# Two matrix products of a graph kernel put into one region, with a shared ring of parts and another order of the second product's tiles

## The chip, the cores and the metric

The kernel runs on one core of one Trainium2 chip. The metric is the device time of one execution in microseconds (us). Three runs of the kernel before gave 911.8, 912.16 and 915.66 us, median 912.16 us.

## What is computed

`x` is 2048 x 512, `adj` is 2048 x 2048, all in fp32. The part of the reference that matters here:

```
def _L0_gnn_ref(x, Coefficient2, A):        # called as _L0_gnn_ref(h, adj, adj)
    def adjacent_mat(adj):
        adj = adj + jnp.eye(adj.shape[0])
        deg = jnp.sum(adj, axis=1)
        dinv = jnp.where(deg > 0, deg ** (-0.5), 0.0)
        return dinv[:, None] * adj * dinv[None, :]
    adj = adjacent_mat((A + A.T) * 0.5)
    y = Coefficient2 @ adj
    y = y @ x
    return y

h = jnp.maximum(_layernorm(x, axis=-1), 0.0)
x = x + _L0_gnn_ref(h, adj, adj)
h = jnp.maximum(_layernorm(x, axis=-1), 0.0)
x = x + _L1_gnn_ref(h, adj, L1_gnn_W, ...)   # 8 heads of masked attention, then four dense layers
return x
```

The kernel takes `Coefficient2 @ (A_norm @ h)` from the right: the **first product** is G = A_norm h (2048 x 512), with A_norm = dinv (A + A.T + 2I)/2 dinv, and the **second product** is adj @ G. Adding `x` to it gives `x1`, which the projection to the heads and the attention use.

## The kernel before, in words

**Tiles.** All 2048-row arrays are 16 tiles of 128 rows (T = 16). Both products sum over 16 tiles, and each is made in two halves of eight output tiles, because eight PSUM banks of 128 x 512 hold eight output tiles (`bank[0..7]`, G8 = 8). A **step** is one tile of the sum times the eight output tiles of a half. To hold fp32 accuracy each factor is split in a high and a low part of type fp32r, and a step is 8 banks x 3 matmuls (lines 73, 74 and 75: high by high, high by low, low by high), 24 matmuls of 128 x 512. Each product has 32 steps.

**Ring of parts.** A step needs four tiles: the high and the low part of the 128 x 1024 rows (`s_hi`, `s_lo` in the first product, `a_hi`, `a_lo` in the second) and of the 128 x 512 tile on the other side (`x_hi`, `x_lo`; `g_hi`, `g_lo`). Each has two buffers, so that the parts of step s+1 are cut while PE works on step s. ACT cuts `s_hi` and `x_hi` (lines 516 and 522) and `a_hi` (748); DVE cuts `s_lo` and `x_lo` (289, 295), `g_hi`, `g_lo` and `a_lo` (816, 818, 821) and writes the 0/1 mask of the rows (823). A step's parts may be cut once the step two before it is done (`slot_free`).

**First product** (`smooth_features`). 20 steps are run while `adj` and its transpose come in. Steps 20 to 31 (`FIRST_LATE` to `STEPS - 1`) need only what lies in SBUF: the tiles `kept` (12 tiles) and `kept_end` (4). The banks of the tiles 8 to 15 of G are taken out at step 20 (line 474), those of the tiles 0 to 7 at the end (line 494). Each is one DVE instruction for one bank, and the one for bank k may run when PE has finished the last step's three matmuls into bank k.

**Border.** Each product is a region of its own (`nc.Block()`): all engines meet at its end, and the second one's code begins after that. The second region's SBUF tiles lie where the first one's were.

**Second product** (`spread_and_project`). The row tiles of the transpose come through `rows`, which has four places (SLOTS = 4). The first four tiles are loaded by the end of the first product's queue. SP (the engine that issues the loads here) first issues x's second load (4 MB, line 717), the weights (719) and two vectors (723), and then, for each further row tile, waits until its place is free (line 729: the mask of the tile four before is done) and loads it (line 87). The tiles are taken in the order 0, 1, ..., 15 in both halves, so step 0 needs tile 0 of G. After the last step of each half DVE adds x to the banks (line 830).

After that come the second layer norm, the projection, and attention with the dense layers, none of which the diff touches.

Of the kernel before, what the change touches and what calls it, by code (L numbers as in the profile page):

```python
# [37 lines left out]
P = 128  # L38
# [63 lines left out]
def smooth_features(nc, bank, ident, G, rows, rows_loaded, x, adj, adj_t):  # L102
# [5 lines left out]
    with ExitStack() as ctx:  # L108
        def sb(name, shape, dt=F32):
            return ctx.enter_context(nc.sbuf_tensor(name, shape, dt))  # L110

        def sem(name):
            return ctx.enter_context(nc.semaphore(name))

        EARLY = SLOTS
        FIRST_NOW = 2 * EARLY
        FIRST_LATE = T + EARLY
        STEPS = 2 * T
        CHUNKS = ((0, 4), (4, 8), (8, 12), (12, 16))
        h = sb("l0_h", [P, T, F])  # L120
        now = sb("l0_now", [P, SLOTS, GW])
        with nc.sbuf_tensor("l0_early_hi", [P, EARLY, F], F32R) as early_hi, \
                nc.sbuf_tensor("l0_early_lo", [P, EARLY, F], F32R) as early_lo:
            pass
        kept_end = sb("l0_kept_end", [P, SLOTS, GW])
        kept = sb("l0_kept", [P, T - SLOTS, GW])
        rows_k = sb("l0_rows_k", [P, SLOTS, GW])
        s_hi = sb("l0_s_hi", [P, 2, GW], F32R)
        s_lo = sb("l0_s_lo", [P, 2, GW], F32R)
        x_hi = sb("l0_x_hi", [P, 2, F], F32R)  # L130
        x_lo = sb("l0_x_lo", [P, 2, F], F32R)
        base = now[:, 0:2, 0:F]
        stats = sb("l0_stats", [P, 4, 6])
        mv = sb("l0_mv", [P, T, 2])
        var = sb("l0_var", [P, T])
        root = sb("l0_root", [P, T])
        rstd = sb("l0_rstd", [P, T])
        nmr = sb("l0_nmr", [P, T])
        tmp = sb("l0_tmp", [P, T])
        part = sb("l0_part", [P, T, 2])  # L140
        deg = sb("l0_deg", [P, T, 1])
        pos = sb("l0_pos", [P, T, 1])
        degc = sb("l0_degc", [P, T, 1])
        droot = sb("l0_droot", [P, T, 1])
        y = sb("l0_y", [P, T, 1])
        ytmp = sb("l0_ytmp", [P, T, 1])
        dinv = sb("l0_dinv", [P, T, 1])
        hdinv = sb("l0_hdinv", [P, T, 1])

        def kept_half(i):  # L150
            return kept[:, i, :] if i < T - SLOTS else kept_end[:, i - T + SLOTS, :]

        ident_zeroed = sem("ident_zeroed")
        x_loaded = [sem(f"l0_x_loaded{c}") for c in range(len(CHUNKS))]
        sums_loaded = [sem(f"l0_sums_loaded{b}") for b in range(SLOTS)]
        first_loaded = sem("l0_first_loaded")
        ln_chain = sem("l0_ln_chain")
        var_ready = sem("l0_var_ready")
        ln_root = sem("l0_ln_root")
        norm_ready = sem("l0_norm_ready")  # L160
        h_ready = sem("l0_h_ready")
        summed = sem("l0_summed")
        inv_chain = sem("l0_inv_chain")
        deg_ready = sem("l0_deg_ready")
        root_ready = sem("l0_root_ready")
        hi_ready = sem("l0_hi_ready")
        lo_ready = sem("l0_lo_ready")
        x_hi_ready = sem("l0_x_hi_ready")
        x_ready = sem("l0_x_ready")
        slot_free = sem("l0_slot_free")  # L170
        acc_done = sem("l0_acc_done")
        part_kept = sem("l0_part_kept")
        base_ready = sem("l0_base_ready")
        g_done = sem("l0_g_done")
        INV = 4
        DEG = 3

        def half_of(i, at_once):
            left = (i < EARLY) == at_once
            return slice(0, GW) if left else slice(GW, N)  # L180

        def step_source(s):
            if s < EARLY:
                return now[:, s, :]
            if s < FIRST_NOW:
                return kept_half(s - EARLY)
            if s < FIRST_LATE:
                return now[:, (s - EARLY) % SLOTS, :]
            return kept_half(s - T)

        def x_of(s):

            if s < EARLY:
                return s, s, early_hi[:, s, :], early_lo[:, s, :]
            return (s - EARLY if s < FIRST_LATE else s - T), s - EARLY, x_hi[:, s % 2, :], x_lo[:, s % 2, :]

        def wait_for_sum(eng, s, k):

            group = (EARLY - 1, FIRST_LATE - 1, STEPS - 1).index(s)
            if k < G8 - 1:  # L200
                eng.wait_ge(acc_done, (G8 - 1) * group + k + 1)
            else:
                eng.wait_ge(slot_free, s + 3)

        with nc.Block() as block:
            @block.sync
            def _(sp):
                def load_x(c):
                    lo, hi = CHUNKS[c]
                    sp.dma_start(h[:, lo:hi, :], x[lo * P:hi * P, :].rearrange("(t p) f -> p t f", p=P)  # L210
                                 ).then_inc(x_loaded[c], 16)

                def load(i):
                    b, tile = i % SLOTS, slice(i * P, (i + 1) * P)
                    first, second = half_of(i, True), half_of(i, False)
                    if i >= SLOTS:
                        before = i - SLOTS
                        sp.wait_ge(deg_ready, DEG * before + 1)
                        sp.wait_ge(lo_ready, (before if before < EARLY else before + EARLY) + 1)
                    sp.dma_start(rows[:, b, :], adj_t[tile, first]).then_inc(rows_loaded[b], 16)  # L220
                    sp.dma_start(now[:, b, :], adj[tile, first]).then_inc(sums_loaded[b] if i else first_loaded, 16)
                    sp.dma_start(rows_k[:, b, :], adj_t[tile, second]).then_inc(sums_loaded[b], 16)
                    sp.dma_start(kept_half(i), adj[tile, second]).then_inc(sums_loaded[b], 16)

                load_x(0)
                for i in range(EARLY + 2):
                    load(i)
# [12 lines left out]
            def _(v):  # L240
                links = {}

                def link(*name):

                    links[name] = len(links) + 1

                def statistics(c):
                    lo, hi = CHUNKS[c]
                    v.wait_ge(x_loaded[c], 16)
                    for t in range(lo, hi):  # L250
                        v.bn_stats(stats[:, t - lo, :], h[:, t, :]).then_inc(ln_chain, 1)
                        link("stats", t)

                def variances(c):
                    lo, hi = CHUNKS[c]
                    for k in range(hi - lo):
                        v.wait_ge(ln_chain, links["stats", lo + k])
                        v.bn_aggr(mv[:, lo + k, :], stats[:, k, :]).then_inc(ln_chain, 1)
                        link("mv", lo + k)
                    v.wait_ge(ln_chain, links["mv", hi - 1])  # L260
                    v.tensor_scalar(var[:, lo:hi], mv[:, lo:hi, 1], EPS, None, ALU.add).then_inc(var_ready, 1)

                def refine(c, n):

                    part_of = slice(*CHUNKS[c])
                    d, at, yy, to = var[:, part_of], root[:, part_of], rstd[:, part_of], tmp[:, part_of]
                    if n == 0:
                        v.wait_ge(ln_root, c + 1)
                        v.reciprocal(yy, at).then_inc(ln_chain, 1)
                        link("refined", c, 0)  # L270
                        return
                    v.wait_ge(ln_chain, links["refined", c, n - 1])
                    if n == 1:
                        v.tensor_tensor(to, yy, yy, ALU.mult).then_inc(ln_chain, 1)
                    elif n == 2:
                        v.tensor_tensor(to, to, d, ALU.mult).then_inc(ln_chain, 1)
# [72 lines left out]
                for n in range(6):  # L349
                    refine(0, n)  # L350
# [1714 lines left out]
```

## Time and profile before

| | |
|---|---|
| profiled execution | 911.92 us |
| its span in the profile | 910.0 us |
| median of three runs | 912.16 us |
| PE busy | 860.6 us (95% of the span) |
| DVE busy | 691.3 us (76%) |
| ACT busy | 411.6 us (45%) |
| POOL busy | 274.9 us (30%) |
| mean granted TensorE clock | 0.983 |

PE is TensorE's matmuls, PEld its weight loads, DVE VectorE, ACT ScalarE, POOL GpSimd and SP SyncE. Times in a row are us from the start of the span. A clock of 1.00 is 2.4 GHz, the upper of two levels; the lower is 1.2 GHz. A PE row's start is measured and its end is modelled, so the pace of matmuls is read from the starts. Tile names stand without their numbers (`l_a_hi` is `l1_a_hi`), and `x` can be the tile `x1`.

### The profile page before, as it was taken

To read this page: it belongs to the slowest core of one execution; us is meant where nothing else is said; L and a number is where in the kernel's file an instruction comes from. 1 tells how busy PE (TensorE), PEld (TensorE's weight loads), DVE (VectorE), ACT (ScalarE), POOL (GpSimd) and SP (SyncE) were. 2 spreads that over 40 slices of the span, in tenths; PEclk is the share of its full clock that TensorE was granted. 3 is DMA by queue.
4 is the path that set the end of the run, shared out by engine and by line. 5 is a ranking of instruction groups with operands and counts; after the bars stand their busy time and mean duration, and the time that the engine had idled before them with its cause. 6 is when DMAs were issued, how large, how long until landed. Compare 5 with 4: busy or idle time off the path is not lost.

```text
span 910.0 us, 15449 instructions
## 1 busy us (share of the span) xinstructions
PE 860.6 (95%) x5144; PEld 754.7 (83%) x5144; DVE 691.3 (76%) x1192; ACT 411.6 (45%) x742; POOL 274.9 (30%) x287
## 2 busy tenths in 40 slices
PE   2999999989999999999599999999999999998997
PEld 1787888868888888778399999999999999997553
DVE  6788985564557775677899999999999999996622
ACT  3535423311111221245286666666666656773331
POOL 0000000000000000066646555555555544573111
PEclk9999999999999999999699999999999999999999
DMA  9969820029232321310050000010010032001142
GB/s 353 406 212 340 351 93 1 0 82 279 100 95 90 113 95 46 126 61 4 26 200 25 23 23 26 25 23 23 24 25 23 23 93 71 13 2 47 46 138 96
DMA packets 36115, 87.36 MB, mean 96 GB/s; under 512 B 7072, under 2 KB 7968, under 8 KB 36064
## 3 DMA queue, kind: packets, MB, share of 16 engines
q1 hardware_dynamic: 35024, 82.46, 26.5%
q0 software_dynamic: 1040, 4.26, 1.2%
q8 instruction: 27, 0.44, 0.2%
q14 instruction: 24, 0.20, 0.1%
HBM read 73.93 MB, written 12.78 MB: 95 GB/s over the span
## 4 chain that ended last, share of the span: by engine, by line
PE 46%; DVE 2%; POOL 1%; ACT 1%; issue 1%; ACTq 0%; POOLq 0%; DVEq 0%
PE bank L1558 25%; PE bank L1582 13%; PE bank L2011 3%; DVE l_q L1243 2%; PE bank L73 1%; PE bank L75 1%; PE bank L74 1%; PE bank L1994 1%; PE bank L2003 1%; PE bank L1973 1%; DVE wh L1924 0%; POOL l_parts L1477 0%; POOL l_o_q L1470 0%; ACT l_mask L1356 0%; POOL l_o_m L1489 0%
## 5 line engine op out<-in xcount | busy, mean ns | idle before, releaser
L1243 DVE SCALAR_TENSOR_TENSOR l_q<-bank,neg_d,mask 128x512 fp32r<-128x512 f32 x512 | 338.7, 742 | 28.2 <-PE bank L1558 27.4
L1558 PE MATMUL bank<-l_parts,l_q 128*128 128x260 f32 x2048 | 253.3, 285 | 8.4 <-DVE l_q L1243 8.4
L1558 PEld LDWEIGHTS bank<-l_parts,l_q 128*128 128x128 f32 x2048 | 250.9, 191 | 8.5 <-issue 8.5
L803 POOL TENSOR_TENSOR l_prod<-wh,l_a 128x512 f32<-128x512 f32 x30 | 36.6, 1240 | 401.2 <-ACT wh L773 401.2
L1356 ACT ACTIVATE l_mask<-mask 128x512 fp32r (+1 forms) x256 | 136.4, 619 | 0.2
L1582 PE MATMUL bank<-l_parts,l_mask 128*128 128x260 f32 x1024 | 129.0, 286 | 0.8 <-ACT l_o_q L1362 0.8
L1582 PEld LDWEIGHTS bank<-l_parts,l_mask 128*128 128x128 f32 x1024 | 127.1, 189 | 1.1 <-ACT l_o_q L1362 1.0
L73 PE MATMUL bank<-l_g_hi,l_a_hi 128*128 128x512 f32 x256 | 100.6, 393 | 4.4 <-DVE l_a_lo L821 4.1
L74 PE MATMUL bank<-l_g_lo,l_a_hi 128*128 128x512 f32 x256 | 100.3, 392 | 0.0
L748 ACT ACTIVATE l_a_hi<-rows 128x1024 fp32r<-128x1024 f32 x32 | 33.9, 1062 | 146.4 <-PE bank L75 123.9
L75 PE MATMUL bank<-l_g_hi,l_a_lo 128*128 128x512 f32 x256 | 100.1, 391 | 0.0
L1362 ACT ACTIVATE l_o_q<-bank 128x260 f32<-128x260 f32 x128 | 49.4, 388 | 105.9 <-PE bank L1558 97.8
L73 PE MATMUL bank<-l_x_hi,l_s_hi 128*128 128x512 f32 x192 | 74.9, 390 | 0.4 <-DVE l_x_lo L295 0.4
L74 PE MATMUL bank<-l_x_lo,l_s_hi 128*128 128x512 f32 x192 | 74.7, 389 | 0.0
L75 PE MATMUL bank<-l_x_hi,l_s_lo 128*128 128x512 f32 x192 | 74.7, 389 | 0.0
L73 PEld LDWEIGHTS bank<-l_g_hi,l_a_hi 128*128 128x128 f32 x256 | 48.4, 189 | 15.7 <-issue 5.6
L816 DVE CAST l_g_hi<-G 128x512 fp32r (+1 forms) x32 | 13.7, 427 | 60.8 <-PE bank L75 60.8
L75 PEld LDWEIGHTS bank<-l_g_hi,l_a_lo 128*128 128x128 f32 x256 | 48.5, 189 | 10.1
L74 PEld LDWEIGHTS bank<-l_g_lo,l_a_hi 128*128 128x128 f32 x256 | 48.5, 189 | 10.0
L73 PE MATMUL bank<-l_early_hi,l_s_hi 128*128 128x512 f32 x64 | 26.2, 409 | 18.5 <-DVE l_early_lo L295 18.4
L1177 POOL TENSOR_TENSOR l_o_m<-l_o_m 128x520 f32<-128x520 f32 x16 | 18.3, 1146 | 82.2 <-ACT l_o_m L1369 82.2
L73 PEld LDWEIGHTS bank<-l_x_hi,l_s_hi 128*128 128x128 f32 x192 | 36.0, 188 | 8.4 <-DVE l_x_lo L295 1.1
(176 smaller groups left out, 1237.1 us busy)
## 6 DMA issues: line engine op xcount, KB each, us to landing
rows<-adj_t SPq DMA_DIRECT2D x48, 512.0 KB, 4.1
l_now<-adj SPq DMA_DIRECT2D x16, 512.0 KB, 7.6
l_rows_k<-adj_t SPq DMA_DIRECT2D x16, 512.0 KB, 8.4
l_src<-e_rows SPq DMA_DIRECT2D x30, 256.0 KB, 3.2
l_kept<-adj SPq DMA_DIRECT2D x12, 512.0 KB, 12.6
wh_store<-wh POOLq DMA_DIRECT2D x1, 4160.0 KB, 15.7
l_h<-x SPq DMA_DIRECT2D x4, 1024.0 KB, 16.2
x<-x SPq DMA_DIRECT2D x1, 4096.0 KB, 14.0
```

The costliest lines, as they stand in the source:

```text
L73: pe.matmul(acc, hi, rhs_hi, start=first, stop=False, skip_group_check=True)
L74: pe.matmul(acc, hi, rhs_lo, start=False, stop=False, skip_group_check=True)
L75: return pe.matmul(acc, lo, rhs_hi, start=False, stop=True, skip_group_check=True)
L748: a.activation(a_hi[:, r % 2, :], rows[:, r, :], ACT.Copy).then_inc(hi_ready, 1)
L803: p.tensor_tensor(per_head(prod[:, b, n, :]), wh[:, t, :, 0:HD], per_head(a_b[:, n, :]), ALU.mult).then_inc(prod_ready, 1)
L1177: eng.tensor_tensor(m_hi, m_hi, m_lo, ALU.add).then_inc(summed, 1)
L1243: v.scalar_tensor_tensor(out=q[:, i, :], in0=bank[S_BANKS[hh]][:], scalar=neg_d[:, i, h:h + 1], in1=mask[:, i, cols], op0=ALU.is_ge, op1=A ...
L1356: a.activation(m_r[:, i % MR, :], mask[:, i, cols], ACT.Copy).then_inc(m_ready, 1)
L1362: a.activation(o_q[hh][:, t, :], bank[Q_BANKS[hh][t]][:, 0:PW], ACT.Copy).then_inc(q_bank_free, 1)
L1558: return pe.matmul(bank[Q_BANKS[hh][t]][:, 0:PW], q[:, i, t * P:(t + 1) * P], parts[pair_slot][:, hh, i, :], start=i == 0, stop=i == T - 1)
L1582: return pe.matmul(bank[M_BANKS[t]][:, 0:PW], m_r[:, i % MR, t * P:(t + 1) * P], parts[pair_slot][:, :, i, BOTH_C], start=i == 0, stop=i = ...
L2011: mm = pe.matmul(self.bank[self.ROW_BANKS[t % 2]][:], self.o3[:, c % 2, k, t * P:(t + 1) * P], self.w4_s[:, k, :], start=k == 0, stop=k == ...
```

## The change

The two products become one region. `smooth_features` no longer opens a block; it returns its code for each engine, and `spread_and_project` runs that code ahead of its own in one block.

- **One ring.** `s_hi, s_lo, x_hi, x_lo` are made once and serve both products (in the second under the names `a_hi, a_lo, g_hi, g_lo`).
- **Order of the tiles.** The second product takes the tiles 8 to 15 first and then 0 to 7, in both halves. The four rows loaded ahead are the tiles 8 to 11. The tiles 8 to 15 of G have been ready since step 20 of the first product.
- **DVE.** The parts of the second product's step 0 are cut (`ahead`) before the eight instructions that empty the banks, those of step 1 right behind them, and only then come the masks of both and the memset of `wh`.
- **PE.** The second product's step 0 waits bank by bank for these eight instructions.
- **Loads.** x's second load waits for the low part of the first product's step 24 (`lo_ready` >= T + G8 + 1), the weights' for that of step 27 (`lo_ready` >= 28).
- **Places in SBUF.** x1 and the weights lie where parts of `kept` are that are done by those steps; `mask` and `wh` have changed places; small tiles lie on the other side.

The core of the diff (the body of the first product's functions is moved by one level and otherwise the same, except as shown):

```diff
-                for b in range(SLOTS):
-                    load_half_rows(sp, rows, rows_loaded, adj_t, 0, b, b)
+        for b in range(SLOTS):
+            load_half_rows(sp, rows, rows_loaded, adj_t, 0, G8 + b, b)
...
+        ahead()
+        v.wait_ge(base_ready, 3 * G8)
+        for k in range(G8):
+            wait_for_sum(v, STEPS - 1, k)
+            v.scalar_tensor_tensor(out=G[:, k, :], in0=bank[k][:], scalar=hdinv[:, k, :],
+                                   in1=G[:, k, :], op0=ALU.mult, op1=ALU.add).then_inc(g_done, 1)
...
+    return (sync, vector, scalar, gpsimd, tensor), lo_ready, slot_free, g_done, ident_made
...
+    first_part, first_lo_ready, first_slot_free, first_g_done, ident_made = first
+    first_sync, first_vector, first_scalar, first_gpsimd, first_tensor = first_part
+    a_hi, a_lo, g_hi, g_lo = ring
...
             @block.sync
             def _(sp):
-
+                first_sync(sp)
+                sp.wait_ge(first_lo_ready, T + G8 + 1)
                 sp.dma_start(x1[:], x.rearrange("(t p) f -> p t f", p=P)).then_inc(x_loaded, 16)
+                sp.wait_ge(first_lo_ready, 2 * T - SLOTS)
                 for k in range(KC):
                     sp.dma_start(w_f[:, k, :, :], w[:, k * P:(k + 1) * P, :].rearrange("h p d -> p h d")
                                  ).then_inc(w_loaded, 16)
...
+                def load_turn(g, j, shift):
+                    for r in range(SLOTS):
+                        sp.wait_ge(lo_ready, T * g + SLOTS * j + r + 1 - SLOTS)
+                        sp.wait_ge(mask_done, T * g + SLOTS * j + r + 1 - SLOTS)
+                        load_half_rows(sp, rows, rows_loaded, adj_t, g, SLOTS * j + r + shift, r)
+
                 for g in range(2):
-                    with sp.Fori(1 - g, T // SLOTS) as j:
...
+                    for j in range(1 - g, HALF_TURNS):
+                        load_turn(g, j, G8)
+                    with sp.Fori(HALF_TURNS, T // SLOTS) as j:
+                        load_turn(g, j, -G8)
...
+                first_scalar(a)
+
+                def cut_first():
+                    for r in range(SLOTS):
+                        a.wait_ge(rows_loaded[r], 16 * (T // SLOTS) + 16)
+                        if r < 2:
+                            a.wait_ge(first_slot_free, 2 * T + r + 1)
+                        a.wait_ge(slot_free, r + 1)
+                        a.activation(a_hi[:, r % 2, :], rows[:, r, :], ACT.Copy).then_inc(hi_ready, 1)
...
             @block.vector
             def _(v):
-                v.memset(wh[:, :, :, HD:HE], 1.0)
...
                 def cut(g, j, r):
-                    i, s, b = SLOTS * j + r, T * g + SLOTS * j + r, r % 2
+                    early = g == 0 and isinstance(j, int) and j == 0 and r < 2
+                    i, s, b = tile(j, r), T * g + SLOTS * j + r, r % 2
+                    if early:
+                        v.wait_ge(first_slot_free, 2 * T + r + 1)
...
-                with v.Fori(0, T // SLOTS) as j:
+                def ahead():
+                    v.wait_ge(first_g_done, G8)
+                    cut(0, 0, 0)
+
+                first_vector(v, ahead)
+                cut(0, 0, 1)
+                mark(0, 0, 0)
+                mark(0, 0, 1)
+                v.memset(wh[:, :, :, HD:HE], 1.0)
+                for s in range(2, G8):
+                    cut(0, s // SLOTS, s % SLOTS)
+                v.wait_ge(first_g_done, 2 * G8)
+                with v.Fori(HALF_TURNS, T // SLOTS) as j:
                     for r in range(SLOTS):
                         cut(0, j, r)
...
                 pe.sem_inc(slot_free, 2)
+                first_tensor(pe)
...
                     for k in range(G8):
+                        if first and g == 0:
+                            pe.wait_ge(first_g_done, G8 + k + 1)
```

**Where the instructions stand now.** On DVE, at the border of the products, before (`l_s_lo` of the first product's last step, then the border):

```order
L289 TENSOR_TENSOR l_s_lo<-l_kept_end,l_s_hi 128x1024
L295 SCALAR_TENSOR_TENSOR l_x_lo<-l_h,l_dinv,l_x_hi 128x512
L494 SCALAR_TENSOR_TENSOR G<-bank,l_hdinv,G 128x512 x8
L205 UNCONDITIONAL_BRANCH
L809 UNCONDITIONAL_BRANCH
L811 MEMSET wh 128x128
L852 UNCONDITIONAL_BRANCH
L852 ISA
L816 ISA
L816 COPY l_g_hi<-G 128x512
L818 TENSOR_TENSOR l_g_lo<-G,l_g_hi 128x512
L821 TENSOR_TENSOR l_a_lo<-rows,l_a_hi 128x1024
```

and after (the ring's names are now those of the first product in both, so `x_hi<-G` is the second product's `g_hi`):

```order
L259 TENSOR_TENSOR s_lo<-l_kept_end,s_hi 128x1024
L264 SCALAR_TENSOR_TENSOR x_lo<-l_h,l_dinv,x_hi 128x512
L787 CAST x_hi<-G 128x512
L789 TENSOR_TENSOR x_lo<-G,x_hi 128x512
L792 TENSOR_TENSOR s_lo<-rows,s_hi 128x1024
L452 SCALAR_TENSOR_TENSOR G<-bank,l_hdinv,G 128x512 x8
L787 CAST x_hi<-G 128x512
L789 TENSOR_TENSOR x_lo<-G,x_hi 128x512
L792 TENSOR_TENSOR s_lo<-rows,s_hi 128x1024
L799 TENSOR_SCALAR mask<-rows 128x1024 x2
L836 MEMSET wh 128x128
```

Three instructions of step 0 have moved ahead of the eight that empty the banks, and the branches of the border are gone.

On SP, behind the first product's last loads, before:

```order
L87 DMA rows<-adj_t 128x1024 [waits l0_summed]
L87 DMA rows<-adj_t 128x1024 x3
L205 UNCONDITIONAL_BRANCH
L714 UNCONDITIONAL_BRANCH [waits barrier_Pool_Activation_PE_DVE_SP_release]
L717 DMA x<-x 128x16x512
L719 DMA l_w<-w 128x8x64 x4
L723 DMA l_a<-a 128x512 x2
```

and after:

```order
L87 DMA rows<-adj_t 128x1024 [waits l0_summed]
L87 DMA rows<-adj_t 128x1024 x3
L665 DMA x1<-x 128x16x512 [waits l0_lo_ready]
L668 DMA l2_w<-w 128x8x64 [waits l0_lo_ready]
L668 DMA l2_w<-w 128x8x64 x3
L672 DMA l2_a<-a1 128x512
L672 DMA l2_a<-a2 128x512
L87 DMA rows<-adj_t 128x1024 [waits l1_mask_done,l1_lo_ready] x4
```

The loads stand in the same order. What releases x's and the weights' is now a low part of the first product, where it was the meeting of all engines.

## Rows read from the trace of the kernel before

**Rows 1.** The page: the span.
```profile
span 910.0 us, 15449 instructions
```

**Rows 2.** Busy time by window around the border (then clock, DMA share, GB/s).
```profile
180.00:190.00 10.00, 10.00 (x46) 8.29 (x45) 3.78 (x4) 3.35 (x4) 0.00 (x0) 1.00 0.00 0
196.00:206.00 10.00, 6.10 (x20) 4.59 (x20) 7.23 (x12) 2.00 (x2) 0.00 (x0) 0.83 0.65 239
206.00:216.00 10.00, 10.00 (x46) 8.28 (x45) 5.36 (x8) 2.12 (x2) 0.00 (x0) 1.00 1.19 306
```

**Rows 3.** Waits of PE: total us, times, longest us.
```profile
PE bank L73 <- DVE l_a_lo L821: 4.1, 2, 3.9
```

**Rows 4.** PE in time: start us, duration us, line, operation, idle before.
```profile
190.83 0.39 PE L75 MATMUL bank<-l_x_hi,l_s_lo 128*128 128x512 f32 x1
...
196.27 0.39 PE L75 MATMUL bank<-l_x_hi,l_s_lo 128*128 128x512 f32 x1
200.56 0.73 PE L73 MATMUL bank<-l_g_hi,l_a_hi 128*128 128x512 f32 x1 [3.90 <-DVE l_a_lo L821]
...
204.05 0.39 PE L75 MATMUL bank<-l_g_hi,l_a_lo 128*128 128x512 f32 x1
...
207.72 0.39 PE L73 MATMUL bank<-l_g_hi,l_a_hi 128*128 128x512 f32 x1
```

**Rows 5.** PE in time, at the second product's step 4.
```profile
223.81 0.39 PE L75 MATMUL bank<-l_g_hi,l_a_lo 128*128 128x512 f32 x1
224.44 0.47 PE L73 MATMUL bank<-l_g_hi,l_a_hi 128*128 128x512 f32 x1 [0.24 <-DVE l_a_lo L821]
```

**Rows 6.** DVE in time, border of the products.
```profile
192.00 5.44 DVE L494 SCALAR_TENSOR_TENSOR G<-bank,l_hdinv,G 128x512 f32<-128x512 f32 x8 [3.21 <-PE bank L75]
197.94 0.17 DVE L811 MEMSET wh<- 128x128 f32 x1 [0.49 <-PEq L205]
198.12 0.43 DVE L816 CAST l_g_hi<-G 128x512 fp32r x1
198.58 0.69 DVE L818 TENSOR_TENSOR l_g_lo<-G,l_g_hi 128x512 fp32r<-128x512 f32 x1
199.19 1.22 DVE L821 TENSOR_TENSOR l_a_lo<-rows,l_a_hi 128x1024 fp32r<-128x1024 f32 x1
200.33 0.69 DVE L823 TENSOR_SCALAR mask<-rows 128x1024 f32 x1
```

**Rows 7.** DVE in time: eight banks of step 20, low parts of steps 21, 24 and 27.
```profile
128.96 5.35 DVE L474 SCALAR_TENSOR_TENSOR G<-bank,l_hdinv,G 128x512 f32<-128x512 f32 x8
134.23 1.21 DVE L289 TENSOR_TENSOR l_s_lo<-l_kept,l_s_hi 128x1024 fp32r<-128x1024 f32 x1
...
148.83 1.23 DVE L289 TENSOR_TENSOR l_s_lo<-l_kept,l_s_hi 128x1024 fp32r<-128x1024 f32 x1 [2.31 <-ACT l_s_hi L516]
...
165.15 1.23 DVE L289 TENSOR_TENSOR l_s_lo<-l_kept,l_s_hi 128x1024 fp32r<-128x1024 f32 x1 [2.31 <-ACT l_s_hi L516]
```

**Rows 8.** ACT in time, last step of the first product; step 4 of the second.
```profile
185.81 1.06 ACT L516 ACTIVATE l_s_hi<-l_kept_end 128x1024 fp32r<-128x1024 f32 x1 [3.77 <-PE bank L75]
...
221.97 1.06 ACT L748 ACTIVATE l_a_hi<-rows 128x1024 fp32r<-128x1024 f32 x1 [7.55 <-DMA rows<-adj_t]
```

**Rows 9.** SP in time: loads behind the border.
```profile
197.72 0.38 SPq L717 DMA_DIRECT2D x<-x  x1
198.15 14.37 SPq L719 DMA_DIRECT2D l_w<-w  x4
212.57 1.62 SPq L723 DMA_DIRECT2D l_a<-a  x2
```

**Rows 10.** Loads: size of one, median us from issue to landing.
```profile
rows<-adj_t SPq DMA_DIRECT2D x48, 512.0 KB, 4.1
x<-x SPq DMA_DIRECT2D x1, 4096.0 KB, 14.0
l_w<-w SPq DMA_DIRECT2D x4, 256.0 KB, 9.3
```

More of the change, by code:

```diff
@@ L627, in in_turns, with spread_and_project, sb @@
                 work(k - lag, (k - lag) % 2)
-def spread_and_project(nc, bank, G, rows, rows_loaded, x1, mask, wh, e, fac, neg_d, ident, x, adj_t, w, a1, a2,
-                       e_rows, x1_store):
+def spread_and_project(nc, first, ring, bank, G, rows, rows_loaded, mask, wh, e, fac, neg_d, ident, x, adj_t, w, a1,
+                       a2, e_rows, x1_store):
+    first_part, first_lo_ready, first_slot_free, first_g_done, ident_made = first
+    first_sync, first_vector, first_scalar, first_gpsimd, first_tensor = first_part
+    a_hi, a_lo, g_hi, g_lo = ring
     with ExitStack() as ctx:
-        def sb(name, shape, dt=F32):
-            return ctx.enter_context(nc.sbuf_tensor(name, shape, dt))
+        def sb(name, shape, dt=F32, side="left"):
+            return ctx.enter_context(nc.sbuf_tensor(name, shape, dt, side=side))
         def sem(name):
             return ctx.enter_context(nc.semaphore(name))
-        a_hi = sb("l1_a_hi", [P, 2, GW], F32R)
-        a_lo = sb("l1_a_lo", [P, 2, GW], F32R)
-        g_hi = sb("l1_g_hi", [P, 2, F], F32R)
-        g_lo = sb("l1_g_lo", [P, 2, F], F32R)
-        stats = sb("l1_stats", [P, T, 6])
-        mv = sb("l1_mv", [P, T, 2])
-        var = sb("l1_var", [P, T])
-        root = sb("l1_root", [P, T])
-        tmp = sb("l1_tmp", [P, T])
-        rstd = sb("l1_rstd", [P, T])
-        nmr = sb("l1_nmr", [P, T])
+        w_hi = sb("l2_w_hi", [P, KC, F], F32R)
+        w_lo = sb("l2_w_lo", [P, KC, F], F32R)
+        x1 = sb("x1", [P, T, F])
+        (w_f,), (prod,) = one_place(nc, ctx, [("l2_w", [P, KC, H, HD], F32)], [("l2_prod", [P, 2, 2, F], F32)])
+        a_b = sb("l2_a", [P, 2, F])
+        sel = sb("l2_sel", [2 * H, 2, P])
+        args = [sb(f"l2_args{k}", [P, T, H]) for k in range(3)]
+        stats = sb("l1_stats", [P, T, 6], side="right")
+        mv = sb("l1_mv", [P, T, 2], side="right")
+        var = sb("l1_var", [P, T], side="right")
+        root = sb("l1_root", [P, T], side="right")
+        tmp = sb("l1_tmp", [P, T], side="right")
+        rstd = sb("l1_rstd", [P, T], side="right")
+        nmr = sb("l1_nmr", [P, T], side="right")
         x_loaded = sem("l1_x_loaded")
@@ L668, in spread_and_project @@
         norm_ready = sem("l1_norm_ready")
-        (w_f,), (prod,) = one_place(nc, ctx, [("l2_w", [P, KC, H, HD], F32)], [("l2_prod", [P, 2, 2, F], F32)])
-        w_hi = sb("l2_w_hi", [P, KC, F], F32R)
-        w_lo = sb("l2_w_lo", [P, KC, F], F32R)
-        a_b = sb("l2_a", [P, 2, F])
         e_t = rows[0:2 * H, 0:2, :].rearrange("p b n -> p (b n)")
         h2 = rows[:, 2, :].rearrange("p (b f) -> p b f", b=2)
-        sel = sb("l2_sel", [2 * H, 2, P])
-        dst_top = sb("l2_dst_top", [P, 1, H])
-        args = [sb(f"l2_args{k}", [P, T, H]) for k in range(3)]
-        top = sb("l2_top", [2 * H, 1])
-        tops = sb("l2_tops", [2 * H, 4])
-        top_w = sb("l2_top_w", [2 * H, P])
+        dst_top = sb("l2_dst_top", [P, 1, H], side="right")
+        top = sb("l2_top", [2 * H, 1], side="right")
+        tops = sb("l2_tops", [2 * H, 4], side="right")
+        top_w = sb("l2_top_w", [2 * H, P], side="right")
         w_loaded = sem("l2_w_loaded")
@@ L723, in _ @@
                     sp.dma_start(a_b[:, n, :], row.to_broadcast([P, F])).then_inc(w_loaded, 16)
-                for g in range(2):
-                    with sp.Fori(1 - g, T // SLOTS) as j:
-                        for r in range(SLOTS):
-                            sp.wait_ge(lo_ready, T * g + SLOTS * j + r + 1 - SLOTS)
-                            sp.wait_ge(mask_done, T * g + SLOTS * j + r + 1 - SLOTS)
-                            load_half_rows(sp, rows, rows_loaded, adj_t, g, SLOTS * j + r, r)
+                def load_turn(g, j, shift):
[3 more added lines that the diff above has]
+                        load_half_rows(sp, rows, rows_loaded, adj_t, g, SLOTS * j + r + shift, r)
+                for g in range(2):
+                    for j in range(1 - g, HALF_TURNS):
+                        load_turn(g, j, G8)
+                    with sp.Fori(HALF_TURNS, T // SLOTS) as j:
+                        load_turn(g, j, -G8)
                 sp.wait_ge(x1_done, T)
@@ L796, in _ @@
             def _(p):
+                first_gpsimd(p)
                 p.sem_inc(prod_ready, 1)
@@ L822, in cut, with mark @@
                                     ALU.subtract).then_inc(lo_ready, 1)
+                    if not early:
+                        mark(g, j, r)
+                def mark(g, j, r):
+                    i = tile(j, r)
                     v.tensor_scalar(mask[:, i, g * GW:(g + 1) * GW], rows[:, r, :], 0.0, None,
@@ L2032, in build @@
         rows_loaded = [smooth.enter_context(nc.semaphore(f"rows_loaded{r}")) for r in range(SLOTS)]
-        smooth_features(nc, bank, ident, G, rows, rows_loaded, x, adj, adj_t)
-        wh = sb("wh", [P, T, H, HE])
-        mask = sb("mask", [P, T, N], U8)
-        with nc.sbuf_tensor("x1", [P, T, F], F32) as x1:
-            spread_and_project(nc, bank, G, rows, rows_loaded, x1, mask, wh, e, fac, neg_d, ident, x, adj_t, w, a1, a2,
-                               e_rows, x1_store)
-            smooth.close()
+        ring = [smooth.enter_context(nc.sbuf_tensor(name, [P, 2, size], F32R, side="right"))
+                for name, size in (("s_hi", GW), ("s_lo", GW), ("x_hi", F), ("x_lo", F))]
+        with ExitStack() as within:
+            places = [sb(name, [P, tiles, size], F32, within) for name, tiles, size in (
+                ("l0_h", T, F), ("l0_rows_k", SLOTS, GW), ("l0_kept_end", SLOTS, GW), ("l0_now", SLOTS, GW),
+                ("l0_kept", T - SLOTS, GW))]
+        with ExitStack() as within:
+            sb("l0_to_kept_end", [P, T * F + SLOTS * GW], F32, within)
+            places += [sb(name, [P, SLOTS, F], F32R, within) for name in ("l0_early_hi", "l0_early_lo")]
+        first = smooth_features(nc, smooth, places, ring, bank, ident, G, rows, rows_loaded, x, adj, adj_t)
+        mask = sb("mask", [P, T, N], U8)
+        wh = sb("wh", [P, T, H, HE])
+        spread_and_project(nc, first, ring, bank, G, rows, rows_loaded, mask, wh, e, fac, neg_d, ident, x, adj_t, w,
+                           a1, a2, e_rows, x1_store)
+        smooth.close()
         attend_and_finish(nc, bank, wh, e, mask, ident, adj, e_rows, fac, neg_d, wh_store, x1_store,
```

916 lines of the change are left out of this document (451 added, 465 removed).

## The prediction

> **What bounds the kernel now.** The span is 910.0 us [rows 1], and PE works through nearly all of it. I read the busy times by window first: inside the first product PE is busy 10.00 of 10 us at clock 1.00, and the one window around the border has 6.10 of 10 us and a mean clock of 0.83 [rows 2]. Next the waits of PE: two waits for `a_lo`, 4.1 us together, the longer 3.9 us [rows 3]. The timeline then gives the place and the true price. The reader is to look at the starts of the matmuls, since their ends are modelled. The last matmul of step 30 starts at 190.83 and that of step 31 at 196.27 [rows 4], so a step lasts 5.44 us and a matmul 0.227. The next matmul could start at 196.50; it starts at 200.56. Its step should last 5.44 us, and step 1 starts at 207.72, 7.16 us later: the first eight matmuls take 3.49 us (200.56 to 204.05) instead of 1.81. The clock is at the lower of its two levels there, after the pause. The third loss is at step 4: a matmul starts 0.63 us after the one before it [rows 5], 0.40 late, and is itself 0.08 longer (0.47 against 0.39); the step's `a_hi` waited for its rows [rows 8]. I take 0.45 us for this stall, between 0.40 and 0.48.
>
> What ends the pause is DVE's chain, not PE: the banks are empty at 197.44 (192.00 + 5.44), then come the border (0.50), the memset, `g_hi`, `g_lo` and `a_lo`, which ends at 200.41 [rows 6]; PE starts 0.15 later.
>
> **The change part by part.**
>
> *The pause (border, order of tiles, parts ahead of the banks).* Tile 8 of G is ready from step 20 on [rows 7], so step 0's parts hang only on their buffer, free when step 30 is done. DVE reacts 0.49 us after the start of the releasing matmul: bank 0's third matmul starts at 191.51 (190.83 + 3 x 0.227), and the first emptying at 192.00 [rows 4, 6]. So `g_hi` starts at 190.83 + 0.49 = 191.32, `g_lo` 0.46 later, at 191.78, `a_lo` 0.61 later, at 192.39, and the next instruction 1.14 later, at 193.53 (the distances are those of the starts in [rows 6]). `a_hi` isn't late: ACT's 1.06 us start when step 30 ends, about 191.25, as at 185.81 one step earlier [rows 8]. So step 0's parts are whole at 193.7, and PE wants them at 196.50.
>
> The eight banks then take 5.27 us, the distance of eight such instructions and the next when none waits (128.96 to 134.23) [rows 7]. They run from 193.53 to 198.80, where they now run from 192.00 to 197.44: 1.4 us later. PE wants bank k at 196.50 + 0.68k. Bank 0 is free at 194.3 and bank 7 at about 198.9, against 196.50 and 201.26. So the second product starts at 196.50 with no pause: 200.56 - 196.50 = **4.06 us** off.
>
> *Step 1.* This is what is late next. After the banks DVE cuts step 1: 198.80 + 0.46 + 0.61 = 199.87, `a_lo` 1.22 long to 201.09, and 0.15 for PE to see it: 201.24. PE wants it at 196.50 + 5.44 = 201.94. The margin is 0.70 us. I cost it at nothing; DVE's two masks and the memset, queued behind, hide in step 1. If each of the eleven instructions from the first bank on were 0.1 us slower, the stall would be 0.4 us. From above, if DVE got through them no faster than PE fills banks (0.68 each, 0.2 us in all), still nothing. I keep 0 to 1.0 us for the range.
>
> *Step 2 and on.* The two masks (0.69 each) and the memset (0.17) end by 202.6, and step 2's parts come 0.46 + 0.61 + 1.22 later, at 204.9; PE wants them at 207.38. In every later step DVE needs 2.9 us (0.46 + 0.61 + 1.14 + 0.69) of 5.44. The unrolled turns add no work.
>
> *The clock.* With no pause the matmuls go on at the pace before. Step 0 takes 5.44 us where it took 7.16: **1.72 us** off. That the pause is what lowers the clock is read from one place; bounds are 0 (it falls anyway) and 1.72, and I take 1.72, because in [rows 2] clocks are 1.00 on both sides and the windows with a continuous PE show no drop.
>
> The Trainium skill ("TensorE: Matmul & The Clock Gate", section "What's actually happening") says that the number of slow matmuls after such a start varies between runs of one kernel, with 6, 11 and 14 as its examples. The trace has 8 here, and no other run is shown. By those counts at the 0.21 us that a slow matmul costs extra here, the term would be an estimated 1.3 to 2.9 us and the time 904.5 to 906.1.
>
> *The loads.* x's load may go when step 24's low part is done, 148.83 + 1.23 = 150.1, the weights' after step 27's, 166.4 [rows 7]. x takes 14.0 us to land, so it is there at 164; the weights and vectors take 14.4 and 1.6 us of SP and land 9.3 after their issue [rows 9, 10]: about 192 at the latest. SP is then free about 10 us before its next duty, the row tile of step 4, which waits for step 0's mask, now at about 201.7. 4.1 us later, at 206, it has landed [rows 10]; ACT wants it when step 2 is done, 196.50 + 3 x 5.44 = 212.8. Before, that load was queued behind x, weights and vectors and came at 221.97 [rows 8]. So the stall of step 4 goes: **0.45 us** off. What the loads run beside now is the first product's end instead of the second's beginning: PE kept 10.00 of 10 us and 46 matmuls with the DMA at its fullest (306 GB/s), the same as with none [rows 2]. I cost them at nothing. They were waited for by nobody before (x by the addition a half later), and are not now.
>
> *The rest* (places in SBUF, one wait more on the identity matrix, POOL's order): nothing. DVE's copy and mask have the same sizes, and the identity is made in the first microseconds.
>
> **Sum.** 4.06 + 1.72 + 0.45 = 6.2 us. Everything behind the border hangs on PE, so the whole of it shifts. The profiled execution took 911.92 us, 1.9 over its span; 911.92 - 6.2 = 905.7. The median shown, 912.16, is 0.2 above the profiled one, so about 905.8 for a median; I say 905.8.
>
> **The rivals.**
>
> 1. *Step 1 is late.* DVE comes to step 1's parts 1.4 us later than without `ahead`, and they follow the banks with a margin of 0.70. For it: DVE has no gap in the plan between 191.3 and 201.1, so any delay reaches PE once it is over 0.70. Against it: all distances come from rows of the same instructions. Price 0.3 to 1.0 us: 906.1 to 906.8. Chance 0.08.
>
> 2. *The clock falls all the same.* If what lowers it is the work, or x's load, rather than the pause, 1.7 us stay: 907.5. Against it: x's load was under way at 206 to 216 too, with clock 1.00 [rows 2]. Chance 0.05.
>
> 3. *The change doesn't do what it says.* PE sees `a_lo` or the banks late, so that part of the pause is left. If DVE's three instructions waited for step 31 instead of step 30, they would start at 196.27 + 0.49 = 196.76; PE would start at 199.2, 2.7 late; the banks would follow from 199.0 to 204.2, and step 1's parts come at 206.7, 2.0 after PE wants them: 910.4. Half of that is 908. The wait is on the count that step 30 gives, so it is unlikely. Chance 0.05.
>
> 4. *Slower.* The loads hold up the last steps of the first product. Place: steps 24 to 31, when x's 4 MB and the weights' 1 MB are written into SBUF beside PE, ACT and DVE. A step has 5.44 us; it becomes slower only when ACT's and DVE's cuts (1.06 + 1.14 + 0.75) or the matmuls grow beyond it. Each of eight steps would have to last 0.78 us more, 14%, to eat the 6.2; at 1 us more the time is 913.7. Against it: [rows 2] again, the same matmul count beside a fuller DMA. Chance 0.03.
>
> **How the numbers follow.** The forecast has 0.79, the rivals 0.08, 0.05, 0.05 and 0.03. A measurement of this kernel tells 0.5%, 4.6 us, from no change, so faster means under 907.6. The forecast, rival 1 and nearly all of rival 2 lie there: 0.90. Rival 3 and the rest give 0.07 for within, rival 4 0.03 for slower. The range: below, a larger saving of slow matmuls by a microsecond, and 0.2 of spread, 904.6; above, rivals 1 and 2 and a median that is read somewhat high (one of the three runs shown is 3.5 above the median), 907.8.
>
> **What would show it.** Right: between the last matmul of the first product and the first of the second 0.23 us, and 5.44 to step 1; the clock in that window 1.00; no wait of PE for the second product's `a_lo`; three DVE instructions ahead of the eight, which run at 0.66 us each from about 193.5; x's load issued at 150; ACT's step 4 waiting for PE, not for rows. Wrong: a wait of PE at step 1 (rival 1), slow matmuls after a seamless border (rival 2), a first matmul later than 197 (rival 3), or steps longer than 5.44 us between 150 and 190 (rival 4).

## Result

Over 11 runs each the changed kernel has a median of 906.91 us (905.17 to 909.93), the kernel before 912.79 us. The ratio is 0.9936, interval 0.9921 to 0.9951: 4.5 to 7.2 us less. 905.8 was forecast, in a range of 904.6 to 907.8. The profiled execution has a span of 903.8 us, against 910.0 [rows 1]; 903.8 is also what 910.0 - 6.2 gives. One of the nine runs of `loads_at_border` below took 2219.06 us and is left out of every comparison; why it did isn't known.

The windows of the changed kernel (busy time of PE, PEld, DVE, ACT, POOL; then clock, DMA share, GB/s):

```profile
150.00:160.00 10.00, 10.00 (x46) 8.26 (x45) 5.31 (x9) 2.84 (x4) 0.00 (x0) 1.00 0.82 305
180.00:190.00 10.00, 10.00 (x46) 8.29 (x45) 3.78 (x4) 3.34 (x4) 0.00 (x0) 1.00 0.00 0
196.00:206.00 10.00, 10.00 (x45) 8.26 (x44) 9.33 (x15) 2.12 (x2) 0.00 (x0) 1.00 0.28 93
```

The window at the border had 6.10 us of PE and clock 0.83 [rows 2]; it is full now. x's load runs in the first window at 305 GB/s, beside as many matmuls as in the second, where nothing is loaded.

PE in time, from the first product's last matmuls to step 1 of the second (in this kernel both products use the ring's names):

```profile
196.26 0.39 PE L74 MATMUL bank<-x_lo,s_hi 128*128 128x512 f32 x1
196.49 0.39 PE L75 MATMUL bank<-x_hi,s_lo 128*128 128x512 f32 x1
196.71 0.39 PE L73 MATMUL bank<-x_hi,s_hi 128*128 128x512 f32 x1
...
202.15 0.39 PE L73 MATMUL bank<-x_hi,s_hi 128*128 128x512 f32 x1
...
218.47 0.39 PE L73 MATMUL bank<-x_hi,s_hi 128*128 128x512 f32 x1
```

From the last matmul to step 1 it is 5.66 us, where it was 11.45 [rows 4]: 5.79 less, and 5.78 was the forecast of the two terms (4.06 and 1.72). The last row is the first matmul of step 4, 6.0 us earlier than the 224.44 of [rows 5]. DVE there:

```profile
191.53 0.43 DVE L787 CAST x_hi<-G 128x512 fp32r<-128x512 f32 x1 [2.51 <-issue]
191.99 0.69 DVE L789 TENSOR_TENSOR x_lo<-G,x_hi 128x512 fp32r<-128x512 f32 x1
192.62 1.23 DVE L792 TENSOR_TENSOR s_lo<-rows,s_hi 128x1024 fp32r<-128x1024 f32 x1
193.76 5.36 DVE L452 SCALAR_TENSOR_TENSOR G<-bank,l_hdinv,G 128x512 f32<-128x512 f32 x8
199.03 0.41 DVE L787 CAST x_hi<-G 128x512 fp32r<-128x512 f32 x1
199.48 0.69 DVE L789 TENSOR_TENSOR x_lo<-G,x_hi 128x512 fp32r<-128x512 f32 x1
200.09 1.22 DVE L792 TENSOR_TENSOR s_lo<-rows,s_hi 128x1024 fp32r<-128x1024 f32 x1
201.22 1.29 DVE L799 TENSOR_SCALAR mask<-rows 128x1024 uint8<-128x1024 f32 x2
```

All of it stands 0.2 us behind the forecast, like PE. Step 1's last part is ready at 201.31, 0.84 before PE takes step 1 at 202.15. SP and ACT:

```profile
150.30 0.38 SPq L665 DMA_DIRECT2D x<-x  x1
166.62 2.92 SPq L668 DMA_DIRECT2D l_w<-w  x4
169.58 1.59 SPq L672 DMA_DIRECT2D l_a<-a  x2
202.00 20.18 SPq L87 DMA_DIRECT2D rows<-adj_t  x6
```

```profile
213.23 1.06 ACT L711 ACTIVATE s_hi<-rows 128x1024 fp32r<-128x1024 f32 x1 [4.32 <-PE bank L75]
```

x's load is issued at 150.3 (150.1 forecast); the weights' four take 2.92 us of SP, not the 14.37 of [rows 9], where they followed x's within half a microsecond. ACT's step 4 waits for PE and no longer for rows [rows 8].

### The profile page after: what moved, and what is told of

Same layout as the page of the kernel before. It is cut to its first block, busy times and chain, and to the rows that moved or that the text cites. A ratio compares the mean times of both kernels' runs of the same rounds, so it can differ in the third digit from the quotient of the medians.

```text
span 903.8 us, 15367 instructions
## 1 busy us (share of the span) xinstructions
PE 856.6 (95%) x5144; PEld 750.9 (83%) x5144; DVE 691.6 (77%) x1192; ACT 411.1 (45%) x742; POOL 275.0 (30%) x287
## 4 chain that ended last, share of the span: by engine, by line
PE 46%; DVE 4%; ACT 1%; issue 0%; ACTq 0%; DVEq 0%
PE bank L1551 25%; PE bank L1575 13%; PE bank L2004 3%; DVE l_q L1236 3%; PE bank L73 1%; PE bank L75 1%; PE bank L74 1%; PE bank L1987 1%; PE bank L1996 1%; PE bank L1966 1%; DVE wh L1917 0%; ACT l_mask L1349 0%; ACT l_enc_t_hi L1939 0%; ACT l_o_q L1355 0%; DVE l_enc_t_lo L1885 0%
## 5 line engine op out<-in xcount | busy, mean ns | idle before, releaser
L73 PE MATMUL bank<-x_hi,s_hi 128*128 128x512 f32 x448 | 174.5, 389 | 0.3 <-PE bank L75 0.3
L74 PE MATMUL bank<-x_lo,s_hi 128*128 128x512 f32 x448 | 174.3, 389 | 0.0
L75 PE MATMUL bank<-x_hi,s_lo 128*128 128x512 f32 x448 | 174.3, 389 | 0.0
L73 PEld LDWEIGHTS bank<-x_hi,s_hi 128*128 128x128 f32 x448 | 84.1, 188 | 18.3 <-issue 0.7
L75 PEld LDWEIGHTS bank<-x_hi,s_lo 128*128 128x128 f32 x448 | 84.1, 188 | 17.6
L74 PEld LDWEIGHTS bank<-x_lo,s_hi 128*128 128x128 f32 x448 | 84.1, 188 | 17.4
L711 ACT ACTIVATE s_hi<-rows 128x1024 fp32r<-128x1024 f32 x28 | 29.7, 1062 | 123.1 <-PE bank L75 118.6
L73 PE MATMUL bank<-l_early_hi,s_hi 128*128 128x512 f32 x64 | 26.4, 412 | 19.0 <-DVE l_early_lo L264 19.0
L792 DVE TENSOR_TENSOR s_lo<-rows,s_hi 128x1024 fp32r<-128x1024 f32 x32 | 39.1, 1222 | 0.0
L1362 ACT ACTIVATE l_o_m<-bank 128x260 f32<-128x260 f32 x64 | 24.8, 388 | 14.7 <-PE bank L1575 10.1
```

The source lines that it names most:

```text
L73: pe.matmul(acc, hi, rhs_hi, start=first, stop=False, skip_group_check=True)
L74: pe.matmul(acc, hi, rhs_lo, start=False, stop=False, skip_group_check=True)
L75: return pe.matmul(acc, lo, rhs_hi, start=False, stop=True, skip_group_check=True)
L711: a.activation(a_hi[:, r % 2, :], rows[:, r, :], ACT.Copy).then_inc(hi_ready, 1)
L792: v.tensor_tensor(a_lo[:, b, :], rows[:, r, :], a_hi[:, b, :].bitcast(F32), ALU.subtract).then_inc(lo_ready, 1)
```

## The experiments

All but the first and `rows_first` are edits of the changed kernel. Spans are those of the profiled executions; for a single run only these are compared. The notes on clocks are gathered behind the last experiment.

### before_again: the kernel before, a second profile

> The kernel before, unchanged, profiled a second time: how much do the pause and the slow matmuls at the border vary from run to run? Theory A (the pause is set by DVE's chain, and the slow matmuls follow from the pause): the pause again 3.9 us within 0.1, slow matmuls 8 give or take 3 (they start to be slow with the pause, their number may differ). Rival (the slow matmuls come from something else that happened in that one execution): none slow, or slow ones elsewhere.

Span 909.2. The border:

```profile
200.56 0.77 PE L73 MATMUL bank<-l_g_hi,l_a_hi 128*128 128x512 f32 x1 [3.90 <-DVE l_a_lo L821]
```

```profile
198.00:203.00 5.00, 2.44 (x6) 1.98 (x7) 4.91 (x8) 2.00 (x2) 0.00 (x0) 0.62 0.73 263
203.00:208.00 5.00, 5.00 (x18) 3.95 (x17) 0.82 (x2) 0.00 (x0) 0.00 (x0) 0.70 1.00 379
```

The pause is the same, 3.90 us. The slow matmuls (those at the lower level of the clock, 0.43 us from start to start) last until 205.82, some 13 instead of 8, and cost 2.6 us instead of 1.7. That is outside the 8 give or take 3 that was expected; the rival falls, since they stand behind the pause again. And step 4 doesn't stall here: PE comes to it later, while its rows land when they did. What the clock takes more, the stall takes less.

### parts_last: step 0's parts behind the banks

```diff
-        ahead()
         v.wait_ge(base_ready, 3 * G8)
         for k in range(G8):
             ...
+        ahead()
```

> The changed kernel with step 0's parts cut behind the eight instructions that empty the banks; tile order, one region and early loads stay. Theory A: banks empty at 197.7, parts ready at 199.9, first matmul of the second product at about 200.1, a pause of 3.4 us, slow matmuls behind it (1.0 to 1.8 us more), no stall at step 4; span 903.8 + 4.4 to 5.2 = 908.2 to 909.0, so about 0.45 to 1.2 us faster than before. Rival (the meeting of the engines at the border is what costs): the span stays within 1 us of 903.8.

Span 908.8; ratio to before 0.9991 (0.9979 to 1.0003), no difference that shows. By the ratios 5.0 of the 5.9 us are gone with this one edit, although region, tile order and early loads are there.

```profile
196.88 0.39 PE L75 MATMUL bank<-x_hi,s_lo 128*128 128x512 f32 x1
200.36 0.47 PE L73 MATMUL bank<-x_hi,s_hi 128*128 128x512 f32 x1 [3.09 <-issue]
```

A pause of 3.25 us beyond the 0.23 us from matmul to matmul (3.4 expected). The rival, that the meeting of the engines is what costs, falls. But no matmul behind the pause was slow:

```profile
203.00:208.00 5.00, 5.00 (x24) 4.14 (x23) 2.67 (x6) 1.06 (x1) 0.00 (x0) 1.00 0.58 210
```

So the span lies in the expected range partly by luck. The pause and what stands before it put this profile 3.7 us behind that of the changed kernel; another 1.1 us are lost only in the window from 825 to 830, where the clock is 0.66 here and 1.00 there.

### parts_last_again: the same, a second profile

> The kernel with step 0's parts behind the banks, profiled a second time. Theory B (the length of the pause decides on the clock): no slow matmul again, as in its first run with the same pause. Theory C (the same pause is followed by slow matmuls in one run and by none in another): slow ones this time in about half of the cases, span up to 911.

The same 3.48 us from matmul to matmul, and this time slow matmuls:

```profile
198.00:203.00 5.00, 3.19 (x10) 2.57 (x11) 4.97 (x7) 0.00 (x0) 0.00 (x0) 0.79 0.00 0
203.00:208.00 5.00, 5.00 (x21) 4.08 (x20) 1.09 (x4) 0.79 (x1) 0.00 (x0) 0.87 0.63 210
```

About 1.6 us are lost in them. The same kernel with the same pause has both outcomes, as theory C says.

### loads_at_border: the loads late, the rest as changed

```diff
-                sp.wait_ge(first_lo_ready, T + G8 + 1)
+                sp.wait_ge(first_g_done, 2 * G8)
                 sp.dma_start(x1[:], ...
```

> The changed kernel, but x's second load (and with it the weights', queued behind it) waits for the last bank to be emptied (about 199) instead of step 24. Theory A: the load of step 4's rows is queued behind them as before and lands at about 223.4, while PE, no longer paused, would want step 4 at 218.5; step 4's parts come at 225.8, a stall of about 7 us with slow matmuls behind it (1 to 1.8): span 903.8 + 8 to 9 = 912 to 913, slower than before. So the early loads are worth far more in this kernel than the 0.45 us that they cost the kernel before. Rival (the loads' place is worth what it cost before): span 904.3.

Span 915.1; ratio 1.0043 (1.0028 to 1.0057), slower than before. PE, ACT and SP:

```profile
225.36 0.77 PE L73 MATMUL bank<-x_hi,s_hi 128*128 128x512 f32 x1 [6.87 <-DVE s_lo L792]
```

```profile
222.89 1.06 ACT L711 ACTIVATE s_hi<-rows 128x1024 fp32r<-128x1024 f32 x1 [14.13 <-DMA rows<-adj_t]
```

```profile
199.00 0.38 SPq L665 DMA_DIRECT2D x<-x  x1
199.42 14.13 SPq L668 DMA_DIRECT2D l_w<-w  x4
```

The border is seamless in this kernel, but PE reaches step 4 seven microseconds before its rows, which are queued behind 5 MB as in the kernel before. The slow matmuls behind that wait are 14 and cost 2.9 us, 1.1 to 1.9 more than expected. Stall and slow matmuls make 9.8 us. The other 1.5 of the 11.3 us between the two spans are lost at the end of the second product, where this profile has two stretches of slow matmuls (at 385 and 402 us) and that of the changed kernel has one (at 390).

### border_only: one region and the ring alone

```diff
-            load_half_rows(sp, rows, rows_loaded, adj_t, 0, G8 + b, b)
+            load_half_rows(sp, rows, rows_loaded, adj_t, 0, b, b)
...     (tiles 0 to 15 in cut, mark and load_turn; loads as in loads_at_border; parts as in parts_last)
```

> One region and the shared ring alone: tiles in the old order, step 0's parts behind the banks, x's load at the border. Theory A: DVE saves the border's 0.5 us, first matmul of the second product at about 200.1 (pause 3.4 instead of 3.9), slow matmuls as before, and step 4 stalls by some 1.0 us, 0.5 more than before since its rows still land at about 222: span 909.5 to 910.2, no change. Rival (one region is the gain): span 905 or less.

Span 913.1; ratio 1.0012 (0.9998 to 1.0026): no gain, but 3 us above the expected span.

```profile
200.32 0.47 PE L73 MATMUL bank<-x_hi,s_hi 128*128 128x512 f32 x1 [3.21 <-issue]
226.10 0.47 PE L73 MATMUL bank<-x_hi,s_hi 128*128 128x512 f32 x1 [2.12 <-DVE s_lo L792]
```

The pause is what was expected. The stall at step 4 is 2.3 us and not 1.0: the rows came at 223.6, 1.7 us later than in the kernel before [rows 8], although SP issued their load at 214.42, 0.2 us earlier. Why they did isn't settled. Another 1.6 us are lost later, again in a second stretch of slow matmuls at the end of the second product (383 and 400 us).

### rows_first: the kernel before, row tiles ahead of x

```diff
+                early_turn(1)     # the rows of steps 4 to 7
                 sp.dma_start(x1[:], x.rearrange("(t p) f -> p t f", p=P)).then_inc(x_loaded, 16)
+                early_turn(2)     # the rows of steps 8 to 11
                 for k in range(KC):
                     ...
```

> The kernel before with only the order of the loads behind the border changed: the rows of the steps 4 to 7, then x, then the rows of the steps 8 to 11, then weights and vectors. Theory A: step 4's rows land long before PE wants them, so no stall there; the pause stays 3.9 us and slow matmuls stay; gain 0 to 0.5 us, no measurable change. Rival (x's load behind the border is what lowers the clock or what DVE's chain suffers from): the pause or the slow matmuls go, and 1.7 us or more is gained.

Span 909.0; ratio 0.9982 (0.9969 to 0.9996), 0.4 to 2.8 us. The stall is gone, pause and slow matmuls (12) are there, so x's load is not what makes them.

```profile
200.49 0.77 PE L73 MATMUL bank<-l_g_hi,l_a_hi 128*128 128x512 f32 x1 [3.90 <-DVE l_a_lo L828]
```

Taking the loads out of the way alone is worth little in the kernel before, though the middle of the interval, 1.6 us, is above the 0 to 0.5 expected. In this profile nothing of it is gained at the border: with 12 slow matmuls step 4 starts at 224.80, not earlier than the 224.44 of [rows 5].

### loads_behind_rows: late loads that are out of the way

```diff
+                load_turn(0, 1, G8)
                 sp.wait_ge(first_lo_ready, T + G8 + 1)
                 sp.dma_start(x1[:], ...
+                load_turn(0, 2, -G8)
                 (weights and vectors)
+                load_turn(0, 3, -G8)
```

> The changed kernel with x's second load behind the loads of the rows of steps 4 to 7 (some 220 us) and the weights' behind those of steps 8 to 11, instead of at steps 24 and 27. Theory A (the loads must only be out of the way of the row tiles): no pause, no stall at step 4 or later, span 903.8 within 0.5. Rival (they must be early): a stall at step 8 or a wait for x at the end of the first half (about 282), 1 us or more.

Span 903.7, ratio 0.9933 (0.9910 to 0.9955), the same as the changed kernel. x's load is issued at 211.14, 60 us later than in the changed kernel, and nobody waits. They needn't be early, only behind the rows.

### old_tile_order: tiles 0 to 15, one bank ahead of step 0's parts

```diff
         for k in range(G8):
+            if k == 1:
+                ahead()
             wait_for_sum(v, STEPS - 1, k)
...
-                    return (SLOTS * j + r + G8) % T
+                    return SLOTS * j + r
...     (the loads likewise; step 1's parts wait for all eight banks)
```

> The changed kernel with the tiles taken in the old order (0 to 15): step 0 needs tile 0 of G, so its parts are cut behind the first of the eight instructions that empty the banks instead of ahead of them. Theory A (PE wants step 0's parts only when step 31 ends, so one bank instruction ahead of them does no harm): parts ready at 195.3, no pause; the rest of the banks is done at the same 199.0, step 1's parts come when they did, PE waits 0 to 0.2 us at step 1: span 903.8 to 904.1. The order of the tiles is then worth nothing by itself. Rival (the order of the tiles is what removes the pause): a pause of 1 us or more.

Span 904.0, ratio 0.9936 (0.9914 to 0.9959), the same as the changed kernel.

```profile
192.11 0.75 DVE L453 SCALAR_TENSOR_TENSOR G<-bank,l_hdinv,G 128x512 f32<-128x512 f32 x1 [3.21 <-PE bank L75]
...
193.97 1.22 DVE L793 TENSOR_TENSOR s_lo<-rows,s_hi 128x1024 fp32r<-128x1024 f32 x1
195.10 4.70 DVE L453 SCALAR_TENSOR_TENSOR G<-bank,l_hdinv,G 128x512 f32<-128x512 f32 x7
...
200.90 1.22 DVE L793 TENSOR_TENSOR s_lo<-rows,s_hi 128x1024 fp32r<-128x1024 f32 x1
```

No pause at the border; step 1 is 0.23 us late and its first matmul 0.08 longer, somewhat more than expected. So in this profile the new order of the tiles is worth at most 0.3 us.

### masks_first: the margin at step 1

```diff
-                cut(0, 0, 1)
+                v.wait_ge(hi_ready, 2)
                 mark(0, 0, 0)
                 mark(0, 0, 1)
                 v.memset(wh[:, :, :, HD:HE], 1.0)
+                cut(0, 0, 1)
```

> The changed kernel, but with both masks and the memset between the eight bank instructions and step 1's parts, 1.37 us more on DVE's chain. Margin read from the changed kernel: a_lo of step 1 ends at 201.31 and PE could take it at 201.46, against 202.15. Theory A: PE waits at step 1, 1.37 - 0.69 = 0.7 us, no slow matmul, span 904.5. Rival (step 1's parts have far more room, or PE waits for something else): no wait, span 903.8.

```profile
201.75 0.39 PE L75 MATMUL bank<-x_hi,s_lo 128*128 128x512 f32 x1
202.65 0.47 PE L73 MATMUL bank<-x_hi,s_hi 128*128 128x512 f32 x1 [0.52 <-DVE s_lo L792]
```

Step 1 is 0.67 us late (0.90 less 0.23) and the span 904.3. So the margin is the 0.7 us that the forecast had, and the order of `cut` and `mark` behind the banks is worth as much.

### parts_after6 and parts_after4: pauses of other lengths

```diff
         for k in range(G8):
+            if k == 6:            # 4 in the other
+                ahead()
             wait_for_sum(v, STEPS - 1, k)
```

> The changed kernel with step 0's parts cut between the sixth and the seventh of the eight instructions that empty the banks. Theory A (PE starts 0.15 us after a_lo): a_lo ends at 198.6 and PE starts at 198.7, a pause of 2.0 us; step 1 not late. Theory B, that the clock falls with every pause at the border: 8 or more slow matmuls, span 907.5; theory C, that it falls by chance of timing, as the run with the parts last (pause 3.3 us, none slow) and the one with one region alone (3.4 us, eight slow, beginning 1.9 us after the start) suggest: anything from none (span 905.8) to a dozen (908.5).

> The changed kernel with step 0's parts between the fourth and the fifth of the bank instructions. By the run with them behind the sixth (PE's first matmul 0.10 us after a_lo ends, pause 1.88 us where 2.0 was forecast), a_lo ends at 197.2 and PE starts at 197.3, a pause of about 0.5 us, and no slow matmul at the border. If slow matmuls follow even so short a pause, the clock's fall doesn't need the engine to be idle for long.

PE starts 1.88 and 0.53 us late, and in neither is a matmul slow there. Theory B falls: a pause at the border needn't lower the clock. Yet the spans are 908.4 and 905.4, more than the pause above 903.8. The rest lies far from the border: 1.6 and 1.1 us in the stretches below for `parts_after6`, 1.0 us in one from 820 to 825 for `parts_after4`. `parts_after6`, where attention starts and where the tail starts:

```profile
456.00:461.00 5.00, 2.98 (x20) 2.68 (x19) 5.00 (x8) 5.00 (x13) 1.72 (x1) 0.92 1.02 392
461.00:466.00 5.00, 5.00 (x34) 5.00 (x33) 4.81 (x8) 4.30 (x7) 0.00 (x0) 0.74 0.95 328
...
825.00:830.00 5.00, 4.75 (x28) 4.54 (x26) 3.75 (x8) 2.98 (x7) 0.00 (x0) 0.66 0.00 0
```

The changed kernel's profile has clock 1.00 in the windows from 456 to 466 and from 820 to 840. Pauses there are in every variant, and whether slow matmuls follow differs from run to run of one kernel too: from 830 to 835 the two profiles of the kernel before have clocks of 0.79 and 1.00.

**The clock, taken together.** Slow matmuls behind the pause at the border: 8 and 13 in two profiles of the kernel before, 12 in `rows_first` (all after 3.9 us of pause), none and some 8 in two profiles of `parts_last` (3.25 us), 8 in `border_only` (3.4), none after 1.88 and 0.53 us, 14 after the 7.0 us of `loads_at_border`. A given pause costs no fixed amount; the longest had the most, and the two shortest, with one run each, had none. What decides in a single run isn't shown.

## Why the prediction was right

- **The pause.** The step "parts ahead of the banks, and 1.4 us of delay for the banks that nobody feels" held to within 0.1 us of PE time, and it is the step that carries the gain: `parts_last` undoes it alone and is no faster than before. Region and ring are only what makes it possible; `border_only` gains nothing. But the step carries the gain only together with the loads. Parts ahead with late loads have a ratio of 1.0043, early loads with the parts behind 0.9991, neither 1.0012, both 0.9936.
- **The margin at step 1.** 0.70 us forecast; `masks_first` puts 1.37 us before it and PE waits 0.67. Rival 1 didn't come true; the margin that it named was right.
- **The clock.** 1.72 us was right for the profile shown, but taken as a fixed amount, and a second profile of the same kernel has 2.6. The Trainium skill ("TensorE: Matmul & The Clock Gate", section "What's actually happening") says of a kernel's start that the number of slow matmuls varies between runs of one kernel. Behind a pause these runs agree: 8 and 13 in the kernel before, none and some eight in `parts_last`. That the two profiles are just the forecast's 6.2 us apart is partly luck: 6.0 come at the border, then slow stretches differ in both directions, and at the last addition of DVE it is 7.2 (905.10 against 897.92); the ends of the spans are 1.0 closer again.
- **The loads.** This term was right in the sum and wrong as a price. The forecast had the stall of step 4 as 0.45 us to be gained beside the others. The rows landed at a time that SP's queue set, so the terms were no independent ones: step 4 starts at the later of the rows and PE. `loads_at_border` against the changed kernel makes it 9.8 us by the ratios (1.0043 and 0.9936) and 11.3 by the two profiles (915.1 and 903.8), part of it slow matmuls behind the new wait. It was in the forecast's own numbers: with the rows where they were, step 4 starts at 224.44 [rows 5], however early PE comes; PE now comes at 196.50 + 4 x 5.44 = 218.26, and the 6.2 us between the two are the whole gain that was forecast. Measured it starts at 218.47, 6.0 us earlier. One reading of this part was off without harm: by the forecast's own numbers SP is free at about 182, some 19 us before its next duty and not 10 (in the trace at 171.2).
- **Rivals 2 and 3.** No matmul behind a seamless border was slow, neither here nor in `loads_behind_rows`, and the first one starts at 196.71, not later than 197. Both fell.
- **Rival 4** (steps 24 to 31 slower beside the loads): 46 matmuls in 10 us at 305 GB/s, as without. It fell.
- **The tile order**, which the forecast took as part of the mechanism, is not needed for it (`old_tile_order`).

No version beat the changed kernel; `loads_behind_rows` and `old_tile_order` equal it.

## What to carry to other kernels

Where one stage's last results are taken out of PSUM by the engine that also prepares the next stage's first operands, prepare first: PE wants the banks one by one while its next step lasts, the operands when it begins. Before counting a removed pause, go down the next steps and ask for each what sets its start besides PE; a transfer that was just late enough to be hidden becomes the bound once PE is early. A row of queued loads needs the order in which they are wanted more than an early start.

## What was not expected of the hardware

- Four loads of the weights, 256 KB each, take SP 2.8 to 3.0 us to issue once x's load, issued 16 us earlier, has landed, 5.0 us right behind a row tile's load (`rows_first`, `loads_behind_rows`), and 14.1 to 14.4 us when x's 4 MB were issued just ahead. What is queued behind such a load waits for SP as well as for its own bytes: in the kernel before SP comes to step 4's rows at 214.62, 16.9 us after it issued x's load.
- The same kernel with the same pause of 3.25 us went on at 2.4 GHz in one run and had some eight matmuls at 1.2 GHz in another; in `parts_last_again` and `border_only` the slow matmuls began 1.0 to 1.5 us after PE had started again (the expectation of `parts_after6` has 1.9 for `border_only`, where the first slow matmul starts at 201.78, 1.5 us after 200.32).
